# Cross attention with grouped heads: where the smooth factor is applied, and which engine normalises the queries

## The reference, cut to what matters

```python
ln_out = _ln(hidden_states, ln_w, ln_b)
q = _ln(_fp8_linear_pertensor(ln_out, wq, wq_scale, q_in_scale).reshape(b, s, g, hpg, d), qln_w, qln_b)
k = _ln(_fp8_linear_pertensor(ln_out, wk, wk_scale, k_in_scale).reshape(b, s, g, d), kln_w, kln_b)
v = _fp8_linear_pertensor(ln_out, wv, wv_scale, v_in_scale).reshape(b, s, g, d)
core = _gqa(q, k, v).reshape(b, s, nh * d)
...
xout = _gqa(qx, kx, vx).reshape(b, s, nh * d)
cat = jnp.concatenate([core, xout], axis=-1)
catq = _div_clamp_fp8(cat, proj_smooth)
return jnp.einsum('bsi,oi->bso', catq, wproj) * (proj_in_scale * proj_w_scale)
```

## Time and profile before

| what | us |
|---|---|
| median of 3 runs | 1847.93 |
| lowest and highest | 1846.61, 1858.82 |
| profiled execution, its own time | 1844.32 |
| its span | 1842.5 |
| PE, DVE, ACT, POOL busy in the whole span | 1555.6, 1333.8, 821.8, 638.0 |

### The profile page before, as it was taken

How to read it: one execution, slowest core, us unless ns; L and a number is a source line. 1 busy time by engine, 2 the same in 40 slices (tenths; PEclk the granted TensorE clock), 3 DMA queues, 4 the chain that set the end, 5 groups by cost and what they waited for, 6 DMA issues and landing times. The chain is left out here.

```text
span 1842.5 us, 29067 instructions
## 1 busy us (share of the span) xinstructions
PE 1555.6 (84%) x9134; PEld 1119.8 (61%) x9134; DVE 1333.8 (72%) x3791; ACT 821.8 (45%) x2363; POOL 638.0 (35%) x750
## 2 busy tenths in 40 slices
PE   4898889795557888888995999998978999889984
PEld 3443344463236677666774887887854555788873
DVE  6899797898868898989887356656564333478777
ACT  3133444573546776766773233332321221345552
POOL 1400021575647778878774201111120001221000
PEclk9899999898669999999998999999998999899996
DMA  4255300200929000000002400000262222522110
GB/s 160 69 148 173 130 1 1 86 2 7 209 104 364 22 1 1 1 2 1 1 1 80 139 1 28 13 12 12 89 192 67 87 87 77 197 91 105 62 40 12
DMA packets 103590, 132.48 MB, mean 72 GB/s; under 512 B 14160, under 2 KB 89136, under 8 KB 99472
## 3 DMA queue, kind: packets, MB, share of 16 engines
q1 hardware_dynamic: 94448, 112.39, 19.3%
q0 software_dynamic: 8992, 18.23, 4.0%
HBM read 85.75 MB, written 46.94 MB: 72 GB/s over the span
## 5 line engine op out<-in xcount | busy, mean ns | idle before, releaser
L2455 PE MATMUL l2fa_psQ<-l2fa_xT,l2f_home 128*128 128x128 f32 x1024 | 123.7, 280 | 6.3 <-DMA l2f_home<-in_L2f_kvT 6.3
L2455 PEld LDWEIGHTS l2fa_psQ<-l2fa_xT,l2f_home 128*128 128x128 f32 x1024 | 120.5, 196 | 8.6 <-DMA l2f_home<-in_L2f_kvT 6.7
L653 POOL TENSOR_TENSOR l0f_diag<-g_identb,l0f_mask 128x1024 bf16<-128x1024 bf16 x16 | 31.9, 2021 | 203.4 <-PE l0f_psA L948 191.6
L3235 POOL TENSOR_TENSOR route_rrms<-route_vrms,g_minus_half 128x1 f32<-128x1 f32 x8 | 5.6, 705 | 268.1 <-DVE route_vrms L3257 268.1
L2952 ACT ACTIVATE l2x_probs<-l2x_psS,l2x_nmax 128x128 f32<-128x128 f32 x256 | 90.9, 376 | 13.7 <-DVE l2x_nmax L2871 13.7
L3824 POOL DMA_INDIRECT routed_rows<-rows,route_slot_of x32 | 31.6, 986 | 181.6 <-DMA rows<-moe_yg 170.3
L2783 POOL TENSOR_TENSOR l2x_vsm<-l2x_vraw,l2x_smooth_row 128x512 f32<-128x512 f32 x64 | 91.8, 1435 | 0.0
L2774 POOL TENSOR_TENSOR l2x_probs<-l2x_probs,l2x_rtotal 128x512 f32<-128x512 f32 x64 | 66.6, 1041 | 69.6 <-DVE l2x_rtotal L2877 69.6
L3645 DVE COPY moe_xgT<-moe_psX 128x256 f32<-128x256 f32 x47 | 20.0, 425 | 91.6 <-PE moe_psX L3754 91.6
L3094 PEld LDWEIGHTS l2x_psS<-l2x_kT,l2x_qT 128*128 128x128 f32 x512 | 65.7, 191 | 23.4 <-issue 22.0
L1591 ACT ACTIVATE l2fa_probs<-l2fa_psS,l2fa_bias 128x128 f32<-128x128 f32 x128 | 45.3, 366 | 76.5 <-DVE l2fa_bias L1575 76.5
(11 more groups left out here) (545 smaller groups left out, 4641.8 us busy)
## 6 DMA issues: line engine op xcount, KB each, us to landing
rows<-g_row SPq DMA_DIRECT2D x1, 18304.0 KB, 60.1
kT_ctx<-l0f_held SPq DMA_DIRECT2D x32, 256.0 KB, 3.6
v_ctx<-l0f_held SPq DMA_DIRECT2D x32, 256.0 KB, 3.7
l3a_kT<-kT_ctx SPq DMA_DIRECT2D x8, 1024.0 KB, 5.1
l3a_v<-v_ctx SPq DMA_DIRECT2D x8, 1024.0 KB, 5.6
l0f_wrow<-in_L_ffn_w SPq DMA_DIRECT2D x24, 256.0 KB, 3.0
moe_xg<-rows SPq DMA_DIRECT2D x47, 128.0 KB, 2.0
rows<-moe_yg SPq DMA_DIRECT2D x47, 128.0 KB, 1.7
```

Of the source, the lines that this page charges most:

```text
L2455: last = nc.tensor.matmul(psQ[bank][:, j, :], w[:, c, h * HD:(h + 1) * HD], xT[u][:, c, :], start=(c == 0), stop=(c == KC - 1))
```

## The change

`scale_values`, `vraw`, `vsm` and `smooth_row` go, with the transfer that fills the row. ACT copies the values straight into `v`, in three buffers, and the product reads one value head for two query heads. The smooth factor is applied in `copy_output`: instead of one copy of 128x512, four activations of 128x128, each with its scale column of `W.inverse` (the channel lies on the partitions there). `on_act(t)` becomes `t % 4 != 0`, so groups 2 and 6 of each sequence are normalised by ACT, in steps 3 and 7, and DVE keeps groups 0 and 4 (steps 1 and 5). `qbias` gets two buffers, and POOL makes it for three groups of four.

```diff
@@ -2671,19 +2671,17 @@
 
-        smooth_row = T.sb("smooth_row", [P, 2 * S1])
         xq = I.xq
...
         kmv, qmv = T.sb("kmv", [P, 2, 4, 2]), T.sb("qmv", [P, 2, 4, 2])
-        kve, qve, qbias = T.sb("kve", [P, 4]), T.sb("qve", [P, 4]), T.sb("qbias", [P, 4])
+        kve, qve, qbias = T.sb("kve", [P, 4]), T.sb("qve", [P, 4]), T.sb("qbias", [P, 2, 4])
         krstd, qrstd = T.sb("krstd", [P, 2, 4]), T.sb("qrstd", [P, 2, 4])
...
         kT = T.sb("kT", [P, 2, 4, P])
-        vraw = T.sb("vraw", [P, 2, 4, HD])
-        vsm = T.sb("vsm", [P, 3, 8, HD])
+        v = T.sb("v", [P, 3, 4, HD])
         nmax, total, rtotal = T.sb("nmax", [P, 2, 4]), T.sb("total", [P, 2, 4]), T.sb("rtotal", [P, 2, 4])
@@ -2696,14 +2694,14 @@
 
-        smooth_loaded, order, pool_order = T.sem("smooth_loaded"), T.sem("order"), T.sem("pool_order")
+        order, pool_order = T.sem("order"), T.sem("pool_order")
         xq_ready, x_turned = I.xq_ready, I.x_turned
...
             T.sem("k_normed"), T.sem("q_normed"))
-        k_turned, q_turned, k_copied, q_copied, v_copied, v_ready = (
-            T.sem("k_turned"), T.sem("q_turned"), T.sem("k_copied"), T.sem("q_copied"), T.sem("v_copied"), T.sem("v_ready"))
+        k_turned, q_turned, k_copied, q_copied, v_copied = (
+            T.sem("k_turned"), T.sem("q_turned"), T.sem("k_copied"), T.sem("q_copied"), T.sem("v_copied"))
         s_ready, max_ready, probs_ready, inverted, normed, turned, pT_ready, o_ready = (
@@ -2715,7 +2713,7 @@
 
-        on_act = lambda t: t % 2 == 1
+        on_act = lambda t: t % 4 != 0
         NEXT_PAIRS = [slice(0, 2), slice(2, 4), slice(4, 6), slice(6, 7)]
@@ -2727,8 +2725,6 @@
             def _(sp):
-                sp.dma_start(smooth_row[:, :], row(W.rows[8:40, :].rearrange("k p -> (k p)"), 2 * S1))\
-                    .then_inc(smooth_loaded, 16)
                 sp.wait_ge(zero_made, 1)
@@ -2756,8 +2752,8 @@
                         o.step(ins)
-                        o.step(nc.gpsimd.tensor_tensor(qbias[:, :], qmv[:, t % 2, :, 0], qrstd[:, t % 2, :], ALU.mult))
-                        ins = nc.gpsimd.tensor_scalar(qbias[:, :], qbias[:, :], -1.0, None, ALU.mult)
+                        o.step(nc.gpsimd.tensor_tensor(qbias[:, t % 2, :], qmv[:, t % 2, :, 0], qrstd[:, t % 2, :], ALU.mult))
+                        ins = nc.gpsimd.tensor_scalar(qbias[:, t % 2, :], qbias[:, t % 2, :], -1.0, None, ALU.mult)
                     ins.then_inc(q_rstd, 1)
@@ -2775,17 +2771,6 @@
 
-                def scale_values(j, g):
-                    at_ = 1024 * (j % QUADS)
-                    if g == 0:
-                        pool.wait_ge(v_copied, j + 1)
-                        wait(pool, o_ready, 2 * j - 4)
-                    nc.gpsimd.tensor_tensor(
-                        vsm[:, j % 3, 4 * g:4 * g + 4, :].rearrange("p (g r) d -> p g r d", r=2),
-                        vraw[:, j % 2, 2 * g:2 * g + 2, :].unsqueeze(2).to_broadcast([P, 2, 2, HD]),
-                        smooth_row[:, at_ + 512 * g:at_ + 512 * g + 512].rearrange("p (g r d) -> p g r d", r=2, d=HD),
-                        ALU.mult).then_inc(v_ready, 1)
-
                 def one(t, n):
@@ -2794,10 +2779,6 @@
                         key_rstd(t)
-                    if t < N and t % 2:
-                        scale_values(t // 2, 0)
-                    elif 2 <= t <= N and t % 2 == 0:
-                        scale_values(t // 2 - 1, 1)
                     if b + 1 < B and i == 5:
@@ -2813,7 +2794,6 @@
                 I.scale(pool, 1, W.in_row)
-                pool.wait_ge(smooth_loaded, 16)
                 steps(one)
@@ -2959,7 +2939,7 @@
                         last = nc.scalar.activation(qn[:, t % 2, j, :], bank(2 * t + 1)[:, j, :], ACT.Identity,
-                                                    bias=qbias[:, j:j + 1], scale=qrstd[:, t % 2, j:j + 1])
+                                                    bias=qbias[:, t % 2, j:j + 1], scale=qrstd[:, t % 2, j:j + 1])
                     last.then_inc(q_normed, 1)
@@ -2981,11 +2961,11 @@
                     act.wait_ge(kv_done, t + 1)
-                    wait(act, v_ready, 2 * (j - 1))
+                    wait(act, o_ready, 2 * (j - 2))
                     if cross(t):
-                        ins = nc.scalar.copy(vraw[:, j % 2, :, :], bank(2 * t)[:, :, :])
+                        ins = nc.scalar.copy(v[:, j % 3, :, :], bank(2 * t)[:, :, :])
                     else:
-                        ins = nc.scalar.activation(vraw[:, j % 2, :, :], bank(2 * t)[:, :, :], ACT.Identity,
+                        ins = nc.scalar.activation(v[:, j % 3, :, :], bank(2 * t)[:, :, :], ACT.Identity,
                                                    scale=W.wscale[:, 3:4])
@@ -2997,7 +2977,11 @@
                     wait(act, cat_ready, n - 1)
-                    nc.scalar.copy(cc[:, n % 2, :, :], psO[:, :, :]).then_inc(cc_ready, 1)
+                    for j in range(4):
+                        h = 8 + 4 * (n % NQ) + j
+                        last = nc.scalar.activation(cc[:, n % 2, j, :], psO[:, j, :], ACT.Identity,
+                                                    scale=W.inverse[:, h:h + 1])
+                    last.then_inc(cc_ready, 1)
 
@@ -3103,11 +3087,11 @@
                 def values(n):
-                    pe.wait_ge(v_ready, n + 1)
+                    pe.wait_ge(v_copied, n // 2 + 1)
                     pe.wait_ge(pT_ready, n + 1)
...
                     for j in range(4):
-                        last = nc.tensor.matmul(psO[:, j, :], vsm[:, n // 2 % 3, 4 * (n % 2) + j, :], pT[:, n % 2, j, :],
+                        last = nc.tensor.matmul(psO[:, j, :], v[:, n // 2 % 3, 2 * (n % 2) + j // 2, :], pT[:, n % 2, j, :],
                                                 start=True, stop=True)
```

## The result

The changed kernel takes 1862.3 us (median of 13 runs) against 1846.8 us before (13 runs): a ratio of 1.008, 95% interval 1.0066 to 1.0093. It is slower by 0.8%, 12 to 17 us; 11 us and a median of 1859 were forecast.

The account below looks back on a forecast made before the run. The prediction took a ring of waits, DVE fullest, as the bound. Sixteen stretches losing 0.7 us each made 11 us, all other terms 0: 1847.9 + 11 = 1859 us, own range 1853 to 1866, 8 in 10 within 1839 to 1880.

Parts of the forecast that it names:

- x: Time from POOL's division to the start of ACT's query normalisation; taken as 3.4 us, ends 3.05 and 3.74.
- the stretch: From DVE's reciprocal of step 3 or 7 to the next step's maxima; forecast 0.7 us longer, 16 times.
- The exponentials: ACT's exponentials of steps 4 and 0, queued behind normalisation and `copy_keys`: 5.69 us after the reciprocal, before 3.82.
- the hand-over from `copy_keys` to PE's turning of the queries: In steps 4 and 0, PE's turning was forecast to start 0.05 us after `copy_keys` ends on ACT.
- The output copy: ACT's `copy_output` as four activations: 0.91 us more per step, 58 us of work, hidden in idle time; 0 on the path.
- POOL's relief at nothing: POOL losing the value scaling, 92.5 us of work, priced at 0; at most 4 us of gain.
- Rival 1: DVE is the bound and each of 16 stretches shortens by 1.27: 20.3 us faster, median 1827.6; chance 0.14.
- Rival 2: DVE's gain and ACT's delay cancel, with x near 2.7: median 1848; chance 0.12.
- Rival 3: ACT's split output copy comes onto the path: 58 us, or 29 on top of 11, 1888; chance 0.14.
- The port rule: DVE's fp8 rounding and POOL's SBUF-reading bias instructions exclude each other; in steps 3 and 7, 17 us instead of 11.
- The sum for the profiled execution: Whole kernel: the profiled execution before, 1844.3 us, plus the forecast loss of 11, giving 1855.3.
- the ring: The third attention layer's cycle of engines waiting for each other, with DVE as its fullest member.

Follow-up runs that it names:

- e1: The changed kernel with groups 2 and 6 normalised on DVE again, the rest of the change kept: 1848.6 us, 0.9996 of the kernel before.
- e2: The kernel before with only groups 2 and 6 moved to ACT and two `qbias` buffers: 1863.7 us, 1.0086 of the kernel before.
- e5: The changed kernel with a third small POOL instruction on the bias in steps 3 and 7: 1870.4 us, 1.0101 of the kernel before.
- e8: The changed kernel with the sum of DVE's fp8 rounding moved to POOL, groups 2 and 6 staying on ACT: 1852.4 us, 1.0006 of the kernel before.
- e4: The changed kernel with the output copied in one 128x512 copy, leaving out the smooth factor: 1862.9 us, 1.0072 of the kernel before.
- e3: The changed kernel with `copy_keys` ahead of the query normalisation on ACT: 1856.6 us, 1.0038 of the kernel before.
- e6: The changed kernel with groups 2 and 6 back on DVE and the fp8 rounding's sum on POOL, subtraction and output projection a step later: 1826.7 us, 0.9855 of before.

## Why the prediction was right, point by point

- **The cause.** The move of groups 2 and 6, and nothing else that the steps show (e1, e2). The forecast put all of its 11 us there.
- **x.** Taken as 3.4 (3.27 to 3.74). Measured 734.42 - 731.05 = 3.37 in step 3, and 3.36 to 3.39 in all steps 3 and 7; e5 shows that the stretch follows x nearly one for one. The reason given for 3.4, that DVE's rounding is over by then, doesn't hold: the first bias instruction does meet it (e8), and without that x would be 3.24. The number was right by a part of luck.
- **The exponentials.** Forecast 5.69 after the reciprocal, measured 736.47 - 730.83 = 5.64. The next reciprocal: 7.24 forecast, 7.19 measured. DVE's idle time: 2.3 forecast, 2.21 measured.
- **The term that was mis-sized** is the hand-over from `copy_keys` to PE's turning of the queries. I had taken 0.05 after the end, as for a normalisation; it is 736.85 - (735.80 + 0.79) = 0.26. With it the maxima come 0.87 later in this sequence, 0.88 or 0.89 by the table's medians, not 0.7. Fifteen such stretches lie between the first and the last reciprocal, which makes 13.3 of the table's 13.8; the other 0.5 comes at the two ends of the stage, where steps 4 and 0 give less back.
- **The output copy** was sized too large: 1.38 until the next instruction was forecast, about 1.0 measured. It is hidden all the same (e4), so this cost the sum nothing; the page's busy time of ACT rose by 52 us (821.8 to 874.1), not by the 80 forecast: 33 by the copy (e1, 58 forecast) and 20 by the move (e2, 22 forecast).
- **POOL's relief at nothing**: right (e1). Its busy time fell by 80 us (638.0 to 558.4), 85 forecast.
- **The rivals.** Rival 1 (DVE gets its time back) needed x = 1.5. Its price was also too high by the prediction's own terms: with x = 1.53 `copy_keys` ends at 3.93 and PE turns the queries at 3.98 instead of 5.12, so a stretch could shorten by 1.14 and not by 1.27, 18 us and not 20.3. Rival 2 needed 2.7. Rival 3 (the copy comes onto the path): ACT in step 3 did come close, 0.23 us idle before the probabilities, but the wait for the bias behind it, 0.99, swallowed it. The terms listed against it add up to 6.5 or 6.6, not 6.7, and steps 3 and 7 took 6.19 and 6.24 before, not 6.8; so ACT had less room than was said. Its exponentials of steps 3 and 4 now start at 728.82 and 736.47; less the two idle times that is 6.43 us of work, more than the 6.19 of the step before. An estimate from these rows: even without the 0.99 for the bias the next reciprocal would stand at 736.47 - 0.99 + 1.55 - 730.83 = 6.20, no sooner than before. So the order of POOL's work is not all that stands between this move and a gain.
- **The port rule** (in the Trainium skill, SBUF — State Buffer, Who interferes with whom) was priced at x = 3.74 and a sum of 17 us. The trace agrees with the rule but not with the price: a bias instruction that starts beside one of DVE's rounding instructions ends 0.05 to 0.10 after it (all 67 in the changed kernel, all 52 in the one before), while beside the maxima, which are no such instruction, it takes its shortest time, 0.20 or 0.23. In steps 3 and 7 only the first of the two meets the rounding, with its last instruction, which costs x 0.13 to 0.15 (e8); the power of step 3 stays at 1.01.
- **Not foreseen**: that a late reciprocal of step 0 is handed on to step 1 even when its maxima are on time (e3). In the changed kernel the maxima of step 0 are late too (by 0.88, the reciprocal by 1.00), so it made little difference.
- **A piece of luck.** The sum for the profiled execution, 1855.3, lies within 1 us of the changed kernel's, 1854.6. These two executions differ by 10.3 us and the medians by 15.5; a single execution can't confirm a sum to 1 us.

## What to carry to other kernels

When work is moved from the busiest engine to an idle one, ask not how full the receiver is but what stands behind the moved work in its queue, and what the moved work waits for. Here 1.27 us left DVE, and ACT's exponentials, for which DVE waits next, came 1.82 us later (5.64 against 3.82 after the reciprocal); ACT stood 0.99 of that time waiting for a third engine. Time freed on an engine that isn't in the ring is worth nothing until it takes over work without a deadline: an instruction whose result is needed only a step later gained 1.4% (e6).

## What the runs showed of the hardware that was not expected

```profile
730.85 1.18 ACT L2982 ACTIVATE l2x_cc<-l2x_psO,cw_inverse 128x128 bf16<-128x128 f32 x4
731.84 0.77 ACT L2968 ACTIVATE l2x_v<-l2x_psP,cw_wscale 128x512 f32<-128x512 f32 x1
```

Four activations of 128x128 from PSUM with a scale column take 1.18 us, with the next instruction 0.99 after the first; with scale and bias columns four took 1.51, the next 1.38 later. One alone is nearly as long in both (0.411 and 0.456 on average), so the first kind overlaps more: the next starts 0.26 after its forerunner, against 0.35. The two kinds differ in the bias column and in what they write (bf16 or f32), and no run separates the two. And the hand-over from ACT to PE at the turning of the queries took 0.05 us behind a normalisation but 0.24 to 0.26 behind `copy_keys`, in steps 4 and 0 alike. PE waits there for several semaphores in turn, the one for the normalisation first; whether the place in that row makes the difference was not tried. One thing more, that a small GpSimd instruction ends 0.05 to 0.10 us after the DVE rounding instruction that was running when it started, is shown under e8 and counted under the port rule.
